# Latent attention block on Trainium2: the exponentials of the second and third score piece as one instruction over two PSUM banks

## The reference, cut to what matters

```python
q_r = jnp.einsum('bshq,hqr->bhsr', q_big, W_qr)
k_r = jnp.einsum('bld,hdr->bhlr', kv_r, W_kr)
scores = jnp.einsum('bhsr,bhlr->bhsl', q_r, k_r)
attn = jax.nn.softmax(scores, axis=-1)
ctx_c = jnp.einsum('bhsl,bld->bhsd', attn, kv_r)
```

## Time and profile before

| | |
|---|---|
| median of 3 executions | 1911.38 us (1908.85 to 1916.75) |
| the profiled execution | 1909.03 us |
| its span, first to last instruction | 1907.8 us |
| latent block, first to last exponential | 774.8 to 1592.0 us |
| mean granted TensorE clock | 0.981 |
| busy: PE, PEld, DVE, ACT, POOL | 93%, 77%, 68%, 57%, 36% |

### The profile page before, as it was taken

How to read it: one execution, slowest core, us unless ns; L and a number is a source line. 1 busy time by engine, 2 the same in 40 slices (tenths; PEclk the granted TensorE clock), 3 DMA queues, 4 the chain that set the end, 5 groups by cost and what they waited for, 6 DMA issues and landing times.

```text
span 1907.8 us, 41954 instructions
## 1 busy us (share of the span) xinstructions
PE 1775.6 (93%) x15624; PEld 1478.5 (77%) x15624; DVE 1289.9 (68%) x3463; ACT 1086.8 (57%) x2750; POOL 685.6 (36%) x674
## 2 busy tenths in 40 slices
PE   7999989889998898699999999999999998898995
PEld 5999977646656776599999999999999997774663
DVE  5677657732237665588888888888888888775222
ACT  5776754212223343488888888888888885431221
POOL 5644322232224422443444334433443341213221
PEclk9999999989999999999999999999999999999998
DMA  4000039023247000000000000000000002402323
GB/s 167 23 1 2 1 131 344 23 87 48 45 101 222 3 3 2 22 12 12 12 12 12 29 12 12 12 12 12 12 12 1 1 2 84 193 2 82 48 46 66
DMA packets 51861, 91.69 MB, mean 48 GB/s; under 512 B 4592, under 2 KB 43632, under 8 KB 49232
## 3 DMA queue, kind: packets, MB, share of 16 engines
q1 hardware_dynamic: 42928, 78.16, 12.3%
q0 software_dynamic: 8160, 10.29, 3.5%
q10 hardware_dynamic: 576, 0.56, 0.1%
HBM read 56.13 MB, written 32.87 MB: 47 GB/s over the span
## 4 chain that ended last, share of the span: by engine, by line
PE 73%; DVE 12%; ACT 6%; issue 3%; POOL 2%; DMA 2%; SPq 0%; ACTq 0%; DVEq 0%; POOLq 0%
PE bank L100 60%; PE bank L2546 10%; DVE a_t L703 2%; ACT d_PT L1338 2%; ACT landing L1338 1%; PE bank L1887 1%; PE bank L1159 1%; DVE a_t L700 1%; PE bank L1866 1%; POOL c_rows L1767 1%; POOL g_rows L1767 1%; DVE tiny L133 1%; PE bank L501 1%; DVE d_nm L1426 1%; DVE X L172 0%
## 5 line engine op out<-in xcount | busy, mean ns | idle before, releaser
L2694 DVE TENSOR_REDUCE e_st<-bank 128x1 f32<-128x496 f32 (+2 forms) x512 | 292.0, 571 | 121.7 <-PE bank L100 120.7
L2631 ACT ACTIVATE e_P<-bank,e_st 128x496 f32<-128x496 f32 (+2 forms) x512 | 307.0, 600 | 95.3 <-DVE e_st L2698 93.5
L2713 DVE TENSOR_TENSOR e_PT_lo<-bank,e_PT_hi 128x512 fp32r<-128x512 f32 (+1 forms) x448 | 287.6, 642 | 1.5 <-ACT e_PT_hi L2646 1.4
L2546 PE MATMUL bank<-ident,e_P 128*128 128x128 f32 (+1 forms) x1664 | 258.4, 274 | 4.2 <-DVE e_PT_lo L2713 3.7
L2646 ACT CAST e_PT_hi<-bank 128x512 fp32r<-128x512 f32 (+1 forms) x448 | 248.3, 554 | 10.9 <-PE bank L2546 6.7
L100 PE MATMUL bank<-e_PT_hi,e_kv 128*128 128x256 f32 (+1 forms) x832 | 249.2, 320 | 0.0
L2546 PEld LDWEIGHTS bank<-ident,e_P 128*128 128x128 f32 (+1 forms) x1664 | 195.0, 140 | 31.3 <-issue 26.5
L100 PE MATMUL bank<-e_PT_lo,e_kv 128*128 128x256 f32 (+1 forms) x832 | 215.6, 280 | 0.0
L100 PE MATMUL bank<-e_KT,e_qk_hi 128*128 128x496 f32 (+2 forms) x512 | 198.9, 389 | 7.2 <-ACT e_P L2631 5.7
L100 PE MATMUL bank<-e_KT,e_qk_lo 128*128 128x496 f32 (+2 forms) x512 | 177.0, 346 | 0.0
L100 PEld LDWEIGHTS bank<-e_PT_lo,e_kv 128*128 128x128 f32 (+1 forms) x832 | 158.4, 190 | 2.5
(11 more groups left out here) (470 smaller groups left out, 4960.1 us busy)
## 6 DMA issues: line engine op xcount, KB each, us to landing
c_wall<-in_c_w SPq DMA_DIRECT2D x8, 1536.0 KB, 19.0
g_wall<-in_g_w SPq DMA_DIRECT2D x8, 1536.0 KB, 19.4
c_rows<-normed SPq DMA_DIRECT2D x9, 1040.0 KB, 12.9
g_rows<-normed SPq DMA_DIRECT2D x9, 1040.0 KB, 13.1
e_stage<-in_e_w SPq DMA_DIRECT2D x16, 416.0 KB, 3.2
c_xs<-c_rows SPq DMA_DIRECT2D x23, 130.0 KB, 2.1
g_xs<-g_rows SPq DMA_DIRECT2D x23, 130.0 KB, 2.1
landing<-in_a_wo SPq DMA_DIRECT2D x2, 1024.0 KB, 6.1
```

Source lines behind the costliest of these rows:

```text
L2546: last = pe.transpose(o[0:rows, c * SEQ + i * P:c * SEQ + (i + 1) * P], p[:, i, k0:k0 + rows], ident[:])
L2631: act.activation(Pm[u % 2][:, i, STARTS[j]:STARTS[j] + n], bank[score_bank[j]][:, 0:n], ACT.Exp, bias=s[:, i, 4:5], accum_out=s[:, i, j:j ...
L2694: last = dve.tensor_reduce(s[:, i, j:j + 1], bank[score_bank[j]][:, 0:PIECES[j]], AX.X, ALU.max)
L2713: dve.tensor_tensor(lo, bank[tb_bank[at % 2]][0:rows, 0:n * SEQ].rearrange("p (c n) -> p c n", c=n), hi.bitcast(F32), ALU.subtract).then_i ...
```

## The change

The exponentials of pieces 1 and 2 become one ACTIVATE with 2 x 496 columns, which reads banks 1 and 2 and writes 992 columns of `Pm`. It stands where that of piece 1 stood, in steps 1 and 5; steps 2 and 6 have none. There are three exponentials per half instead of four, three row sums instead of four, and the counts of `exped` follow: scores of pieces 1 and 2 of the next half both wait for the joint instruction.

```diff
+            EXPS, EXP_OF = 3, (0, 1, 1, 2)
...
                         if s >= 4:
-                            pe.wait_ge(*exped.at(s - 3))
+                            pe.wait_ge(*exped.at(EXPS * (2 * u + i - 1) + EXP_OF[j] + 1))
...
-                        pe.wait_ge(*exped.at(8 * u + 8))
+                        pe.wait_ge(*exped.at(EXPS * 2 * (u + 1)))
...
                         act.wait_ge(*maxed.at(2 * u + i + 1))
-                        n, s = PIECES[j], st[u % 4]
-                        act.activation(Pm[u % 2][:, i, STARTS[j]:STARTS[j] + n], bank[score_bank[j]][:, 0:n], ACT.Exp,
-                                       bias=s[:, i, 4:5], accum_out=s[:, i, j:j + 1]).then_inc(*exped.up())
+                        n, s, e = PIECES[j], st[u % 4], EXP_OF[j]
+                        if j == 1:
+                            dst = Pm[u % 2][:, i, STARTS[1]:STARTS[3]].rearrange("p (a n) -> p a n", a=2)
+                            src = psum[:, score_bank[1]:score_bank[2] + 1, 0:n]
+                        else:
+                            dst, src = Pm[u % 2][:, i, STARTS[j]:STARTS[j] + n], bank[score_bank[j]][:, 0:n]
+                        act.activation(dst, src, ACT.Exp, bias=s[:, i, 4:5],
+                                       accum_out=s[:, i, e:e + 1]).then_inc(*exped.up())
...
-                            if u is not None:
+                            if u is not None and j != 2:
                                 exponential(u, half, j)
...
-                        dve.wait_ge(*exped.at(8 * u + 4 * i + 4))
-                        dve.tensor_reduce(s[:, i, 5:6], s[:, i, 0:4], AX.X, ALU.add).then_inc(link.sem, 1)
+                        dve.wait_ge(*exped.at(EXPS * (2 * u + i + 1)))
+                        dve.tensor_reduce(s[:, i, 5:6], s[:, i, 0:EXPS], AX.X, ALU.add).then_inc(link.sem, 1)
```

## The result

The changed kernel takes 1962.91 us (median of 4 executions, 1959.76 to 1965.69), the kernel before, executed beside it, 1914.07 us. The ratio is 1.0249, with a 95% interval of 1.0201 to 1.0296: slower by some 49 us (the two medians alone give 1.0255, inside the interval). The forecast was 1962.

The account below looks back on a forecast made before the run. PE's program with its waits was taken to bound the kernel; 26.9 + 25.2 = 52 us on 1909.0 gave 1961, 1963.5 on the median, stated as 1962. Own range 1950 to 1972; 1934 to 1978 with the first rival.

Parts of the forecast that it names:

- Which wait ends last: Steps 1 and 5: PE's load for score piece 1 follows the second exponential's end, already waiting in 1, 0.02 us margin in 5.
- The length of the joint instruction: Steps 1 and 5: 496 more columns at 0.85 ns add 0.42 us, making the joint activation about 1.10 us.
- The upper end: Joint instruction no better than two apart, its read 0.72 us later; as a rival 90 us, 2001, chance 0.05.
- The two terms: Step 1: 64 units x 0.42 = 26.9 us; step 5: 63 x 0.40 = 25.2 us, both slower.
- What moves along: Behind PE's later score, DVE's lower part and ACT's `upper_qk` move too, so step 3's 0.24 us wait stays.
- the first rival: Only one wait pays (step 1 alone, 1938) or step 3's wait gives back 15 us (1948); chance 0.14.
- The copy behind the joint instruction: `upper_pt` in steps 1 and 5 starts 0.42 us later; costs nothing, as DVE's start moves too.
- ACT's saving: ACT gains 0.24 us a half, 1.14 for 1.38 us; `upper_qk` waits for PE, so the kernel gains nothing.
- One sign that the prediction gave: ACT's idle time before its first exponential should stay as it is.
- The third rival: Steps 1 to 3: ACT sets the pace; 0.24 us in each of 127 halves, 30 us faster, 1881; chance 0.05.
- The clock: PE's clock might fall as it idles more, costing time; grouped with the double-price rival, chance 0.05 together.
- The fourth rival: Gain and loss cancel or the later signal finds slack, needing 0.8 us a unit on PE; 1911, chance 0.04.

Follow-up runs that it names:

- apart: Kernel before with the change's ACT order, but second and third exponentials as two instructions with their own signals: ratio 1.0004, block -0.3 us.
- j_first: Kernel before with the joint exponential only in the first half of each unit (steps 0 to 3): ratio 1.0162, block +29.6 us.
- j_second: Kernel before with the joint exponential only in the second half of each unit (steps 4 to 7): ratio 1.0126, block +24.5 us.
- the two orders moved behind: Kernel before, no joint; group 0's copy behind step 1's second exponential, group 6's lower part behind step 7's maximum: ratio 0.9882, block -20.6 us.
- its control: Kernel before with pieces of 304, 495, 401 and 401 columns and four separate exponentials: ratio 1.0076, block +13.4 us.

## Why the prediction was right

- *Which wait ends last.* The argument was that the second exponential's signal sets PE's time in steps 1 and 5, with a margin of 0.02 us in step 5. `apart` shows it for both together: the same order with piece 1's own signal loses nothing. `j_first` and `j_second` show it for each.
- *The length of the joint instruction.* Taken from the copy over three banks: 681 + 420 = 1101 ns; measured 1098. The upper end, as slow as two, is out.
- *The two terms.* 26.9 and 25.2 us were forecast; in the changed kernel the stretches that end in steps 1 and 5 grew by 26.5 and 25.5, and the block by 51.6 for 52.1. The runs with one half each have 29.6 and 24.5 in the block; in the first, 26.5 of it is step 1, and what the other 3 us in steps 2 and 4 are is not shown.
- *What moves along.* DVE's lower part and ACT's `upper_qk` kept their distances to what releases them (0.59, and 0.04 to 0.05), so the wait ahead of step 3 did not shrink, and the first rival, part of the delay taken back, is out.
- *The copy behind the joint instruction* costs nothing: `apart` has it 0.23 later still.
- *ACT's saving is worth nothing.* The pair took 1.38 us of ACT and the joint instruction 1.08, not 1.14 (1230.03 to the copy at 1231.11), so the saving was 0.30 in the half shown for the 0.24 forecast; it became idle time ahead of `upper_qk` and of the next first exponential. One sign that the prediction gave did not come: ACT's idle time ahead of its first exponential was to stay, and it grew from 93.5 to 116.4 us in all. It says only that ACT had still more time to spare, and does not bear on the sum. The Trainium skill's rule on large tiles ("Advanced Engine Details and Errata", "The Read-Write Bubble") agrees with the trace for ACT's own time, 37 us less busy; what it would make of the kernel's time, a gain of 30 us, did not come. The third rival, that ACT sets the pace, is out.
- *The clock.* 1.00 in the same stretch; it played no part there.
- *No cancelling.* The fourth rival needed 0.8 us of slack a unit. The sum of the two orders moved behind shows that some 0.32 us (20.6/64) was there to be had, in steps 0 and 1, but not for this.
- *What was luck.* That 1962 and 1962.91 agree within 1 us. The executions of the changed kernel alone spread over 6 us, and the kernel before, run beside it, had a median 2.7 us above the one that the forecast started from. The difference of the two profiled executions, 52.1 us, is the better test: the two terms add to 52.1 as well, while single stretches came out up to 2 us off.

## What to carry to other kernels

Joining two instructions joins their signals: the first buffer comes back when the last is done, later by the length of the second part, and this is paid in full wherever the next writer of the first buffer is already waiting or comes just in time. Before joining, look for the start of the consumer against the end of the signal (0.05 us in steps 1 and 5 here: it follows the signal) and against the load before it (0.31 in step 1: it waits; the usual 0.11 in step 5: it does not wait yet, but has nothing to spare). Where it is so tight, rather shorten what stands ahead of that signal. Join where the first bank has slack and the last is waited for: over banks 2 and 3 the same joining was 13 us faster than its control. The same reordering only pays if the thing moved back has slack of its own, so look up who wants it, in every step it is moved in.

## What the runs showed that I had not expected

- A chain over PE alone, with PE "busy" 640 of 640 us, still held waits that two changes of order could remove: 4768 to 4893 matmuls in the same time. Matmuls queued early are drawn over short waits, and the distances of weight loads show them.
- Two exponentials over one bank each, back to back, start 0.66 us apart (1202.76 and 1203.42), and the one over two banks takes 1098 ns; so joining saves ACT 0.23 us on such a pair (1.31 to the next instruction for 1.08), and the first bank comes back 0.41 later (1.20 after the start for 0.79). For a buffer that is waited for, the exchange is a bad one.
- Moving 96 columns from one score piece to a later one, with the same columns in all, cost 13.4 us. The sizes of the pieces are as much a part of this schedule as their order, and they decide which orders pay: moving the lower part behind the maximum brought 9.4 us with the old sizes and nothing with the new.
